# Four of 32 column tiles per phase get their bias from GpSimd

## The reference

```
# layer 0
xn   = (x - mean) / sqrt(var + eps) * gamma          # over the channels
q, k, v = split(w_qkv @ xn)                          # 8 heads of 32
sim  = q^T k * 32**-0.5 + bias[head]                 # 1024 x 1024 per head and element
out0 = w_out @ (softmax(sim) @ v) + x
# layer 1, on out0
f, g, h = Wf @ x + bf, Wg @ x + bg, Wh @ x + bh      # 32, 32, 256 channels
y    = gamma * (h @ softmax(f^T g)) + x
```

## Time and profile before

| | us |
|---|---|
| median of 3 runs (lowest to highest) | 1788.33 (1781.52 to 1788.56) |
| profiled execution, its own time | 1790.26 |
| its span | 1788.5 |
| TensorE busy | 1589.6 (89%) |
| VectorE busy | 1477.8 (83%) |
| ScalarE busy | 1382.2 (77%) |
| GpSimd busy | 7.1 (0%) |
| 512 bias adds of the column phases (L1019) | 597.8, 1216 ns each |
| 512 exponentials of the column phases (L836) | 536.8, 1057 ns each |
| mean granted clock of TensorE | 0.934 |

### The profile page before, as it was taken

The page is one execution under the profiler, slowest core; times in us unless marked ns, Lnnn a source line. Parts: engine busy times, 40 slices in busy tenths (PEclk is TensorE's granted clock), DMA queues, the critical chain, the costliest instruction groups (busy, mean ns, idle before and its releaser), DMA issues.

```text
span 1788.5 us, 18614 instructions
## 1 busy us (share of the span) xinstructions
PE 1589.6 (89%) x5976; PEld 753.9 (42%) x5976; DVE 1477.8 (83%) x2168; ACT 1382.2 (77%) x2033; POOL 7.1 (0%) x5
## 2 busy tenths in 40 slices
PE   6078899899998999889998999989998999999988
PEld 2043335345353544435453443535444453535424
DVE  3067988898988989898888989899889989899853
ACT  2067889788888878878787888878798887889743
POOL 1000000000000000000000000000000000000000
PEclk9577869999999999999999999999999999999999
DMA  5941204320350203501151203502043203400100
GB/s 129 248 138 36 59 1 132 93 59 1 100 148 1 60 1 107 142 25 35 48 165 37 59 1 107 142 1 60 25 124 101 60 1 90 136 1 0 39 10 23
DMA packets 57257, 122.71 MB, mean 69 GB/s; under 512 B 21428, under 2 KB 22964, under 8 KB 57160
## 3 DMA queue, kind: packets, MB, share of 16 engines
q1 hardware_dynamic: 54344, 115.37, 23.5%
q10 hardware_dynamic: 2816, 6.16, 1.3%
HBM read 78.92 MB, written 44.13 MB: 69 GB/s over the span
## 4 chain that ended last, share of the span: by engine, by line
PE 51%; DVE 24%; issue 18%; DMA 3%; ACT 3%; DVEq 0%; ACTq 0%; SPq 0%
DVE biased L1005 13%; PE psum L527 9%; PE psum L602 9%; PE psum L629 8%; PE psum L581 6%; PE psum L407 6%; DVE biased L1019 5%; PE psum L582 4%; PE psum L450 4%; DMA q_stack<-q_parts 2%; PE psum L460 2%; PE psum L484 1%; ACT probs L836 1%; DVE probs L931 1%; DVE x L954 1%
## 5 line engine op out<-in xcount | busy, mean ns | idle before, releaser
L1005 DVE CUSTOM_DVE_ANT_0 biased<-psum,bias_lines_sb 128x1024 f32<-128x1024 f32 x512 | 617.1, 1222 | 174.1 <-PE psum L582 163.0
L819 ACT ACTIVATE biased<-biased,nmax 128x1024 f32<-128x1024 f32 x512 | 587.4, 1148 | 162.5 <-DVE nmax L1005 157.9
L836 ACT ACTIVATE probs<-biased 128x1024 f32<-128x1024 f32 x512 | 536.8, 1057 | 128.6 <-DVE biased L1019 107.5
L1019 DVE TENSOR_TENSOR biased<-psum,bias_lines_sb 128x1024 f32<-128x1024 f32 x512 | 597.8, 1216 | 45.7 <-PE psum L602 33.4
L602 PE MATMUL psum<-q_stack,k_stack 98*128 98x512 f32 x1024 | 392.8, 490 | 38.5 <-DVE nmax L1005 15.9
L581 PE MATMUL psum<-k_stack,q_stack 96*128 96x512 f32 x512 | 331.1, 647 | 102.5 <-DMA q_stack<-q_parts 46.8
L602 PEld LDWEIGHTS psum<-q_stack,k_stack 98*128 98x128 f32 x1024 | 178.9, 200 | 328.8 <-issue 150.8
L629 PE MATMUL psum<-probs,vT 128*32 128x512 f32 x2048 | 285.1, 627 | 6.2 <-DVE st L886 3.9
L581 PEld LDWEIGHTS psum<-k_stack,q_stack 96*128 96x128 f32 x512 | 100.0, 195 | 287.1 <-DVE nmax L1005 165.8
L582 PE MATMUL psum<-k_stack,q_stack 96*128 96x512 f32 x512 | 210.8, 412 | 0.0
L527 PE MATMUL psum<-probs 128*128 128x512 f32 x384 | 186.6, 592 | 0.0
(11 more groups left out here) (78 smaller groups left out, 1090.9 us busy)
## 6 DMA issues: line engine op xcount, KB each, us to landing
q_stack<-q_parts SPq DMA_DIRECT2D x90, 256.0 KB, 5.3
k_stack<-k_parts SPq DMA_DIRECT2D x45, 512.0 KB, 7.3
q_parts<-st SPq DMA_DIRECT2D x15, 1024.0 KB, 3.9
k_parts<-st SPq DMA_DIRECT2D x15, 1024.0 KB, 4.3
xn<-in_x_dram SPq DMA_DIRECT2D x8, 1024.0 KB, 8.9
x<-in_x_dram SPq DMA_DIRECT2D x8, 1024.0 KB, 9.6
out_dram<-x SPq DMA_DIRECT2D x8, 1024.0 KB, 4.1
bias_lines_sb<-bias_lines SPq DMA_DIRECT2D x32, 240.0 KB, 15.1
```

The lines of the kernel that those rows point to most:

```text
L819: nc.scalar.activation(biased[:, m % BIASED, :], biased[:, m % BIASED, :], ACT.Exp, scale=-1.0, bias=nmax[:, m:m + 1], accum_out=rowsum[:, ...
L836: nc.scalar.activation(probs[:, n % P_SLOTS], biased[:, n % BIASED, :] .rearrange("p (i n) -> p i n", i=2), ACT.Exp).then_inc(SEMS["probs_ ...
L1005: nc.vector.tensor_tensor_reduce(biased[:, m % BIASED, :], pair(bank_of(g, first, ("rows", m))), bias_lines[:, g * HG + h, a0:a0 + N], -1. ...
L1019: nc.vector.tensor_tensor(biased[:, n % BIASED, :].rearrange("p (i n) -> p i n", i=2), psum[:, bank:bank + 2, :], bias_lines[:, g * HG + 2 ...
```

## The change

Of the 32 column tiles of each phase, those in `BY_POOL` (4, 11, 18, 25) no longer go through VectorE. ScalarE copies their scores out of PSUM into a new SBUF tile `held`, which is one tile deep; GpSimd adds the bias to it in place; and ScalarE takes the exponential from there. The copy of tile n stands in ScalarE's order ahead of the exponential of n-1, the exponential of n behind that of n+2. So ScalarE's order around tile 4 is: copy 4, exponential 3, 5, 6, 4, 7. TensorE's order is unchanged: PV waits until all `probs` of its pair are made, in the new order (`probs_made`), and a PSUM slot is free when its tile is read by VectorE or copied (`psum_read`). VectorE's slots of `biased` are counted over its own 28 tiles. To make room, `shift_rows` no longer has a tile of its own but lies in the last 32 partitions of `fg_stack`'s.

```diff
 HP = HG // 2
+BY_POOL = (4, 11, 18, 25)
...
-        shift_rows = sb("shift_rows", [HG * NT, NHALF, P], F32R)
         biased = sb("biased", [P, BIASED, N])
+        held = sb("held", [P, 2, HALF])
-        fg_stack = sb("fg_stack", [KS, 2, N], F32R)
+        fg_all = sb("fg_stack", [P, 2, N], F32R)
+        fg_stack = fg_all[0:KS]
+        shift_rows = fg_all[KS:KS + HG * NT, 0, 0:NHALF * P].rearrange("p (r n) -> p r n", n=P)
         nmax1 = sb("nmax1", [P, NT])
         l1 = sb("l1", [P, NT])
...
@@ -284,9 +288,31 @@
-        def last_in_slot(n):
-
-            return SN - (SN - 1 - n) % BIASED
+        BY_DVE = tuple(n for n in range(SN) if n not in BY_POOL)
+
+        def exps_at(n):
+
+            return ([] if n in BY_POOL else [n]) + ([n - 2] if n - 2 in BY_POOL else [])
+
+        EXPS = [m for n in range(SN) for m in exps_at(n)]
+
+        def psum_read(eng, b, g, n):
+            if n in BY_POOL:
+                need(eng, "s_copied", b, g * len(BY_POOL) + BY_POOL.index(n) + 1)
+            else:
+                need(eng, "bias_added", b, g * len(BY_DVE) + BY_DVE.index(n) + 1)
+
+        def columns_read(eng, b, g):
+            psum_read(eng, b, g, BY_POOL[-1])
+            psum_read(eng, b, g, BY_DVE[-1])
+
+        def probs_made(eng, b, g, upto):
+
+            need(eng, "probs_ready", b, g * SN + max(EXPS.index(n) for n in range(upto)) + 1)
+
+        def last_in_slot(slot, count):
+
+            return count - (count - 1 - slot) % BIASED
 
         def split(g, t, half=NHALF - 1):
 
...
@@ -542,17 +568,17 @@
                     elif kind == "turn":
                         need(pe, "rows_ready", b, g * NHALF + n + 1)
                     else:
-                        need(pe, "bias_added", b, g * SN + n + 1)
+                        psum_read(pe, b, g, n)
                 elif item[0] == "rows":
 
-                    need(pe, "bias_added", b, g * SN - (2 if bank_of(g, first, item) == 0 else 1))
+                    psum_read(pe, b - 1 + g, 1 - g, SN - (3 if bank_of(g, first, item) == 0 else 2))
                 elif g == 0:
                     if last:
                         need(pe, "lo_ready", b, split(1, 1))
...
@@ -624,7 +650,7 @@
                                 need(pe, "o_ready", b, half + 1)
                                 if not last:
                                     need(pe, "lo_ready", b + 1, split(0, 1 - half))
-                        need(pe, "probs_ready", b, g * SN + (q - PV_LAG + 1) * HP)
+                        probs_made(pe, b, g, (q - PV_LAG + 1) * HP)
                         for h in range(HG):
                             mm = pe.matmul(psum[h * HD:(h + 1) * HD, 4 + half, :],
                                            vT[:, t, (g * HG + h) * HD:(g * HG + h + 1) * HD],
@@ -827,15 +853,25 @@
                             do(kind, arg, e, g, first, last)
                     do("ln", 1, b, g, first, last)
                     for n in range(SN):
-                        need(act, "bias_added", b, g * SN + n + 1)
-                        if n >= P_SLOTS:
-                            need(act, "pv_mm", b, g * TG + (n - P_SLOTS) // HP + 1)
-                        elif n == 0:
-                            need(act, "pv_mm", b, g * TG)
-                            need(act, "sa_mm", b - 2 + g, NT)
-                        nc.scalar.activation(probs[:, n % P_SLOTS], biased[:, n % BIASED, :]
-                                             .rearrange("p (i n) -> p i n", i=2),
-                                             ACT.Exp).then_inc(SEMS["probs_ready"], 1)
+                        if n + 1 in BY_POOL:
+                            need(act, "s_mm", b, g * SN + n + 2)
+                            bank = bank_of(g, first, ("columns", n + 1))
+                            nc.scalar.copy(held[:], psum[:, bank:bank + 2, :]).then_inc(SEMS["s_copied"], 1)
+                        for m in exps_at(n):
+                            if m in BY_POOL:
+                                need(act, "held_ready", b, g * len(BY_POOL) + BY_POOL.index(m) + 1)
+                                src = held[:]
+                            else:
+                                i = BY_DVE.index(m)
+                                need(act, "bias_added", b, g * len(BY_DVE) + i + 1)
+                                src = biased[:, i % BIASED, :].rearrange("p (i n) -> p i n", i=2)
+                            if m >= P_SLOTS:
+                                need(act, "pv_mm", b, g * TG + (m - P_SLOTS) // HP + 1)
+                            elif m == 0:
+                                need(act, "pv_mm", b, g * TG)
+                                need(act, "sa_mm", b - 2 + g, NT)
+                            nc.scalar.activation(probs[:, m % P_SLOTS], src,
+                                                 ACT.Exp).then_inc(SEMS["probs_ready"], 1)
                         if n == SN // NHALF + (PV_LAG + 1) * HP - 1:
                             output(b, g, 0, last)
                         for kind, arg, e in side_work(g, "columns", n, b, first, last):
@@ -850,6 +886,18 @@
         @block.gpsimd
         def _(pool):
             nc.gpsimd.memset(k_stack[KS:KS + 2].bitcast(F32), 1.0).then_inc(ones_set, 1)
+
+            def element(b, first, last):
+                for g in range(G):
+                    for i, n in enumerate(BY_POOL):
+                        half, t, j = column_tile(n)
+                        a0 = (half * (H // NHALF) + ROWS * t) * W
+                        need(pool, "s_copied", b, g * len(BY_POOL) + i + 1)
+                        nc.gpsimd.tensor_tensor(held[:], held[:],
+                                                bias_lines[:, g * HG + 2 * j:g * HG + 2 * j + 2, a0:a0 + HALF],
+                                                ALU.add).then_inc(SEMS["held_ready"], 1)
+
+            batches(element)
...
@@ -1010,16 +1058,18 @@
                     for n in range(SN):
                         half, t, j = column_tile(n)
                         a0 = (half * (H // NHALF) + ROWS * t) * W
-                        need(dve, "s_mm", b, g * SN + n + 1)
-                        if n >= BIASED:
-                            need(dve, "probs_ready", b, g * SN + n - BIASED + 1)
-                        else:
-                            need(dve, "sum_ready", b, g * A_TILES + last_in_slot(n))
-                        bank = bank_of(g, first, ("columns", n))
-                        nc.vector.tensor_tensor(biased[:, n % BIASED, :].rearrange("p (i n) -> p i n", i=2),
-                                                psum[:, bank:bank + 2, :],
-                                                bias_lines[:, g * HG + 2 * j:g * HG + 2 * j + 2, a0:a0 + HALF],
-                                                ALU.add).then_inc(SEMS["bias_added"], 1)
+                        if n in BY_DVE:
+                            i = BY_DVE.index(n)
+                            need(dve, "s_mm", b, g * SN + n + 1)
+                            if i >= BIASED:
+                                need(dve, "probs_ready", b, g * SN + EXPS.index(BY_DVE[i - BIASED]) + 1)
+                            else:
+                                need(dve, "sum_ready", b, g * A_TILES + last_in_slot(i, A_TILES))
+                            bank = bank_of(g, first, ("columns", n))
+                            nc.vector.tensor_tensor(biased[:, i % BIASED, :].rearrange("p (i n) -> p i n", i=2),
+                                                    psum[:, bank:bank + 2, :],
+                                                    bias_lines[:, g * HG + 2 * j:g * HG + 2 * j + 2, a0:a0 + HALF],
+                                                    ALU.add).then_inc(SEMS["bias_added"], 1)
                         for kind, arg, e in side_work(g, "columns", n, b, first, last):
                             do(kind, arg, e, g, first, last)
 

```

More of the change, by code:

```diff
@@ L162, in two_layer_attention @@
                       shifted=2 * G * NHALF, split_hi=G * NHALF,
-                      parts_ready=G * NHALF, bias_added=G * TG * HP, x1_ready=KC * NHALF, fg_lo=3, h_ready=NT,
+                      parts_ready=G * NHALF, bias_added=G * (TG * HP - len(BY_POOL)), x1_ready=KC * NHALF, fg_lo=3, h_ready=NT,
                       nmax1_ready=NT, rl1_ready=NT, y_ready=KC * NHALF)
@@ L166, in two_layer_attention @@
                       sum_ready=G * HG * NT, ln_ready=2 * G * NHALF,
-                      rows_ready=G * NHALF, probs_ready=G * TG * HP, o_ready=G * NHALF, fg_hi=3, e1_ready=NT, hs_ready=NT)
-        for kind in (TENSOR, VECTOR, SCALAR):
+                      s_copied=G * len(BY_POOL), rows_ready=G * NHALF, probs_ready=G * TG * HP, o_ready=G * NHALF, fg_hi=3, e1_ready=NT, hs_ready=NT)
+        POOL = dict(held_ready=G * len(BY_POOL))
+        for kind in (TENSOR, VECTOR, SCALAR, POOL):
             for name, n in kind.items():
@@ L428, in do @@
                         if t == 0:
-                            need(pe, "bias_added", b, 0)
```

(9 more changed lines are left out.)

## The result

The changed kernel takes 1849.33 us (median of 4 runs, 1848.22 to 1852.88) against 1788.07 for the one before in the same comparison: ratio 1.0355, 95% interval 1.0327 to 1.0383, +61 us. Its profiled execution took 1848.22 us, the span 1846.3. Among the executions of the kernel before that e9 to e12 are compared with is one of 1805.7 us at a granted clock of 0.892, which widens the intervals there and lowers the ratios a little.

The account below looks back on a forecast made before the run. With VectorE relieved, TensorE was taken as the bound. Stalls less gains, +1.1 us per g = 1 and +0.4 per g = 0 phase, gave +12; clock +8 made +20, a 1808 us median; full range 1766 to 1838.

Parts of the forecast that it names:

- rival 1: g = 0 shift: VectorE operations with two SBUF operands stand until GpSimd's add ends; +21 us, 1829 us, chance 0.22.
- The moved exponential: TensorE stands at PV products waiting for late exponentials: 2.9 us per g = 1 phase, 2.2 per g = 0 phase.
- the rule of 0.86 us per quantum: TensorE's side products: each quantum between scores and PV product gives back 0.86 us of a stall.
- The clock: TensorE's granted clock drops behind the tile 25 stall: 0 to 1 us in all 16 phases, half taken, +8 us.
- The copies and GpSimd's time: Column phases: four ScalarE copies, 3.6 us, fit its free time; GpSimd's add, taken as 2.7 us, is hidden.
- the g = 1 phase less its gain: ScalarE's room in a g = 1 column phase: 39.3 us of work beside 41.6 us.
- at least 3.4: Time in us from the copy's end to the late exponential's turn, within which GpSimd's add is hidden.
- The merged tile ..., the doubled waits ... and the wait sums cost nothing: shift_rows' merged tile, waits before h, s1 and q, and wait sums ask for semaphores long set: 0 us.
- later than 9.3 us into the phase: Sign for rival 1: the g = 0 phase's turn starts later than 9.3 us into it.
- the relief: Four VectorE tiles fewer per column phase gain 1.8 us in each of 16 phases, 29 us.
- the gain of 1.1 us forecast for this place: g = 0 turn: the shift's parts come up to 1.13 us earlier, cutting TensorE's 1.22 us wait by 1.1.
- TensorE's 0.66 us wait: g = 0, first product of the second half: wait for a low part of k0, taken as gone, gaining 0.66 us.

Follow-up runs that it names:

- e9: Changed kernel with only the g = 0 column phase's shift moved behind tile 3 and ahead of norm: 1830.9 us, ratio 1.0233.
- e12: Changed kernel with tiles 4, 10, 18, 24, exponentials one tile later, row tiles' slots from 1 on, shift ahead of norm: 1785.3 us, 0.9992.
- e7: Changed kernel without copies and GpSimd adds (four tiles lack bias), exponentials in order from PSUM, row tiles' slots from 1 on: 1764.9 us, 0.9886.
- e4: Changed kernel without GpSimd adds and copies; the four tiles' exponentials read PSUM in order, without bias: 1780.6 us, 0.9973.
- e3: Changed kernel without GpSimd adds (four tiles lack bias), copies kept, exponentials back in their own order: 1779.2 us, 0.9969.
- e2: Changed kernel without GpSimd's 64 adds (those tiles get no bias), copies and late exponentials kept: 1827.4 us, 1.0249.
- e1: Changed kernel with only the row tiles' slots of biased turned, from 1 on: 1840.8 us, 1.0322.
- e8: Changed kernel's late exponentials alone; VectorE adds all 32 biases, no copies and no GpSimd: 1852.2 us, 1.0362.
- e10: Changed kernel with tiles 4, 10, 18, 24 (each first of its pair) in place of 4, 11, 18, 25: 1827.5 us, 1.0209.
- e11: Changed kernel with tiles 5, 11, 17, 25 (each second of its pair) in place of 4, 11, 18, 25: 1882.9 us, 1.052.
- e13: Kernel before the change with only the row tiles' slots from 1 on, so the slot collision alone: 1806.7 us, 1.0098.
- e6: Changed kernel with late pairs' PV one pair later, row tiles' slots from 1 on, and g = 0 shift ahead of norm: 1786.9 us, 1.0009.
- e5: Changed kernel with the PV product of pairs 2, 5, 9, 12 one pair later in TensorE's order: 1840.6 us, 1.0297.

## Why the prediction was wrong, step by step

The sign and the main mechanism held, the size did not: forecast +20, measured +61. The ladder e7, e4, e3, e2, changed kernel splits it (differences of ratios times 1787):

| term | forecast | measured |
|---|---|---|
| four VectorE tiles less, in e7's form | -29 | -20 |
| slot collision | 0 | +16 |
| copies on ScalarE, against e4's form | 0 | -1 |
| late exponentials, stalls and clock | +41 and +8 | +50 |
| GpSimd beside VectorE | 0 (rival 1: +21) | +19 |
| sum | +20 | +64 |

The sum is 63 before rounding; the medians alone give 61. Each step is measured with the ones below it in place, and in another order a step has another size, as e1 shows for the slots.

- **The moved exponential** was sized rightly. Forecast for g = 1: tiles 4, 11, 18, 25 at 0, 0.45, 0.65, 1.8 us; measured in all elements but the last 0, 0.37, 0.77, 1.89. For g = 0, tiles 18 and 25: 0.9 and 1.3; measured 0.77 and 1.22. e3, e8, e10 and e11 show that place and order make it. One part was luck: by the rule of 0.86 us per quantum the stall at tile 11 would be 1.8 - 0.86 = 0.94 us, and no working stands behind the 0.45.
- **The clock** term was taken at half of 1 us in all 16 phases, 8 us. Behind tile 25 it came in six g = 1 phases, 1.3 to 1.9 us each, some 9 us; the size is right, the places were not foreseen, and why the same wait is followed by it in one phase and not in another is open.
- **The copies and GpSimd's time** don't show in the total (e4 with the caution given there, e2). One figure on ScalarE's room was wrong: the g = 1 phase less its gain is 42.3 - 1.8 = 40.5 us, not 41.6. 2.39 us for the add lies under my 2.7. Half of what the Trainium skill's GPSIMD Engine Reference (Elementwise — side-by-side cycle accounting) gives for 2048 elements, an estimate of 2.25, was nearer. The room for it was overstated: from the copy's end to the late exponential of tile 25 it is 3.07 us in g = 1 (1134.55 to 1137.62), not "at least 3.4", which still hides the add.
- **First failed step: "The merged tile ..., the doubled waits ... and the wait sums cost nothing: they ask for semaphores long set, ...".** I checked which semaphore each wait names and not which tile it stands for. 28 tiles in three slots end in slot 0, 32 ended in slot 1, and row tile 0 uses slot 0. L1053's 18.0 us are that wait. e13 shows its price with nothing else changed, 17 to 19 us, and e4 against e7 15 to 17. Taken out of the changed kernel by itself (e1) it gives back 6 to 8: there most of the time is lost again to a wait for TensorE.
- **Second failed step: GpSimd's block stood at nothing in the sum.** Rival 1 had it, as 8 x 2.6 = 21 us on top of the forecast, 1829 us, with a chance of 0.22; but the block and the late exponential don't exclude each other, and both came. Its time and place were right: the add from 994.22, the sign "later than 9.3 us into the phase" met with 9.94, the price 17 to 22 us in e9 and 19 to 22 in e2. The victims were partly others than named: L967 (before: L919) in three phases and in five the copy L972, which has one SBUF operand. I gave it 0.22 because no row showed both engines at once, though the Trainium skill's SBUF — State Buffer (Who interferes with whom) states it for two SBUF operands. With it the sum would have been +41, 1829 us, inside the range; with the collision +57.
- **Third, a mis-sized term: the relief.** 29 us came to 20 to 22 in e7, and e7 is not the relief alone. In it ScalarE's exponential of tile 4 reads PSUM, and the turn takes that tile's PSUM slot. From a g = 0 phase of e7, VectorE, ScalarE, TensorE:
```profile
954.54 0.17 DVE L965 TENSOR_TENSOR shift_parts<-shift,shift_hi 128x16 f32<-128x16 f32 x1
...
954.25 1.00 ACT L870 ACTIVATE probs<-psum 128x1024 f32<-128x1024 f32 x1
...
955.31 0.41 PE L592 MATMUL psum<-ident,shift_parts 128*32 128x128 f32 x2 [1.78 <-ACT probs L870]
```
  The parts of the shift are there at 954.71, the exponential ends at 955.25, and TensorE stands until then. Over the run it waits 8.0 us at the turn for this exponential, as long as it waited before for the shift (7.8). So the gain of 1.1 us forecast for this place is not to be seen in e7, and what the relief is worth by itself is not shown. In g = 1, where the turn does not wait, the six middle phases take 42.3 us on average against 43.1 before: 0.8 each, forecast 1.8 (from e7's profiled execution, which took 1774.6 us, 10 above its median). Why it is so little there stays open. In g = 0 I also took TensorE's 0.66 us wait at the first product of the second half for gone. In the changed kernel it is 0.89 in six phases, and in e4 and e7, which have no copy, it is nil. That ScalarE's copy of tile 18, ahead of exponential 17, is the reason is read from the order, not tried alone.
- **The range** ended at 1838, 9 us above rival 1's 1829. GpSimd's block was inside it. What carries the time past it is the slot collision, which stood in no case, and the relief that came short; the spread of the forecast's own terms, 14 us upward, was not put on rival 1 either.
- What stays open: why e6 regains more (62 us) than e1, e5 and e9 singly (6 to 8, 9 to 10, 17 to 22). By the profiled executions e5 shortens the eight g = 1 column phases from 371.7 to 348.6 us together and lengthens those of g = 0 from 404.6 to 416.8, while e6 has 333.6 and 378.5. So the later product by itself lengthens the g = 0 phases, and no run has the other two repairs without it. The chain over `probs` slots, score slots and PV can hide one wait behind another; I have not taken it apart.

## What to carry to other kernels

When an instruction is moved back in one in-order engine, find its consumer's place in that engine's order and add up the chain from the last common point: here the same move costs 0 to 2 us by whether the tile is first or second of its pair and whether other work lies between. When a count of tiles changes, take it modulo the ring's slots at every border to the next user: an index alone cost 17 to 19 us (e13). And where two costs can occur together, sum them; a case that excludes nothing is a term and not a rival. A run that leaves work out can also change who frees a slot; read its waits before its time is taken as a price.

## What the runs showed of the hardware

- Beside an add of GpSimd (two SBUF reads, 2.36 to 2.41 us) VectorE operations on 16 elements stood until its end, 2.21 to 2.40 us in place of 0.17: L967, with two SBUF operands, and L972, a plain copy with one. One or the other was held in each g = 0 phase; together (0.370 - 0.175) x 32 + (0.499 - 0.175) x 32 = 16.6 us. VectorE's adds of PSUM and SBUF beside it stayed at 1.21 to 1.23. The Trainium skill's SBUF — State Buffer (Who interferes with whom) says that an operation with two SBUF inputs contends with GpSimd's reads, and that a copy or a cast can contend too, since it can enter a 2-port mode. That second part, which my prediction left out, is the one that bears on L972. The trace agrees in who was held and how long; in which mode the copy ran it does not show.
- TensorE's granted clock (levels 1.2 and 2.4 GHz) was 0.50 to 0.65 over 3.7 us behind a wait of 1.89 us in six g = 1 phases, and 1.00 behind the same wait in the other two and in the last g = 0 phase (1665.38), and behind 1.21 us (1033.1). Before the change it was 0.58 behind a wait of 1.22 us. No length of a single wait separates these cases.
